# A graph layer and a sparse expert layer in one launch: first pairs in an order written out by hand, three scatter slots, and a pair placed in its gate's turn

## The reference

```
xn  = layernorm(x)
h   = xn @ W.T + b;  s1 = h @ a1;  s2 = h @ a2
att = sigmoid(s1[i] + s2[j] + att_b) * adj * mask[i] * mask[j]
att = att / (sum_j att + 1e-8)
x   = x + (att @ h) * mask
xn2 = layernorm(x)
w, e = softmax(top2(xn2 @ gate_w + gate_b))           # two of 16 experts
moe = sum over the two: w * (relu(xn2 @ w1[e] + b1[e]) @ w2[e] + b2[e])
out = x + layernorm(xn2 + moe) * gamma + beta
```

## Time and profile before

| | |
|---|---|
| median of 3 runs | 467.93 us (465.33 to 468.48) |
| span of the profiled execution | 466.4 us |
| its own time | not given apart from the span, which lies 1.5 us below the median |
| busy: PE, PEld, DVE, ACT, POOL | 341.8, 282.4, 304.0, 221.8, 311.9 us |
| first scatter, last scatter issued | 50.7, 213.8 us |
| first load of expert rows issued | 220.7 us |

### The profile page before, as it was taken

How to read it: one execution, slowest core, us unless ns; L and a number is a source line. 1 busy time by engine, 2 the same in 40 slices (tenths; PEclk the granted TensorE clock), 3 DMA queues, 4 the chain that set the end, 5 groups by cost and what they waited for, 6 DMA issues and landing times.

```text
span 466.4 us, 11731 instructions
## 1 busy us (share of the span) xinstructions
PE 341.8 (73%) x2259; PEld 282.4 (61%) x2259; DVE 304.0 (65%) x1456; ACT 221.8 (48%) x592; POOL 311.9 (67%) x346
## 2 busy tenths in 40 slices
PE   2787798978798826300799999888898899806991
PEld 1576677867797725200687777777777778702330
DVE  3989897986979948430366666666555555601985
ACT  2578798888889643300233334333333334501441
POOL 6642777777777777673177777777777777760565
PEclk9999998997979965555799999999999999955997
DMA  6912345544645632296867777778777776318983
GB/s 182 325 70 98 114 166 160 174 157 165 187 153 189 224 131 102 103 252 201 220 185 205 210 222 218 220 218 220 216 225 206 231 223 173 82 34 318 334 294 136
DMA packets 61962, 87.97 MB, mean 189 GB/s; under 512 B 10503, under 2 KB 41149, under 8 KB 61780
## 3 DMA queue, kind: packets, MB, share of 16 engines
q1 hardware_dynamic: 32660, 44.89, 33.7%
q0 software_dynamic: 10720, 25.32, 15.2%
q10 hardware_dynamic: 18528, 17.19, 12.4%
HBM read 55.61 MB, written 32.73 MB: 189 GB/s over the span
## 4 chain that ended last, share of the span: by engine, by line
PE 26%; ACTq 16%; DVE 15%; issue 13%; DMA 9%; ACT 9%; SPq 6%; POOL 3%; DVEq 1%; POOLq 0%
PE psum L1187 7%; ACTq L564 6%; ACTq L277 5%; PE psum L1176 5%; ACTq L276 5%; ACT hid L569 4%; DMA sorted_x<-xrow,rows 3%; PE psum L1092 3%; DMA out_dram<-z 2%; PE psum L1110 2%; DVE z L1016 2%; DMA w_sb<-w_dram 2%; ACT xn L520 2%; DVE xmid L729 1%; POOL sorted_x L414 1%
## 5 line engine op out<-in xcount | busy, mean ns | idle before, releaser
L436 POOL DMA_INDIRECT token_y<-yb,xb x143 | 143.4, 1002 | 60.2 <-issue 38.7
L414 POOL DMA_INDIRECT sorted_x<-xrow,rows x128 | 123.4, 964 | 41.7 <-issue 39.1
L569 ACT ACTIVATE hid<-psum,b_sb 128x256 f32<-128x256 f32 (+1 forms) x188 | 69.3, 419 | 140.2 <-PE psum L1176 60.0
L1187 PE MATMUL psum<-w_sb,hid 128*128 x572 | 83.2, 283 | 12.0 <-ACT hid L569 11.9
L1187 PEld LDWEIGHTS psum<-w_sb,hid 128*128 128x128 f32 x572 | 74.5, 191 | 22.0 <-issue 19.3
L1176 PE MATMUL psum<-xbT,w_sb 128*128 128x256 f32 (+1 forms) x376 | 81.9, 341 | 2.1 <-DVE xbT L966 1.9
L975 DVE TENSOR_TENSOR yb<-psum,b_bc 128x256 f32<-128x256 f32 x94 | 33.9, 360 | 62.8 <-PE psum L1187 51.2
L1176 PEld LDWEIGHTS psum<-xbT,w_sb 128*128 128x128 f32 x376 | 57.6, 193 | 7.6 <-DVE xbT L966 4.2
L1166 PE MATMUL psum<-ident_aug,xb 128*128 128x128 f32 x143 | 33.3, 290 | 23.2 <-DMA xb<-sorted_x 21.2
L980 DVE SCALAR_TENSOR_TENSOR yb<-yb,xb 128x128 f32<-128x128 f32 x143 | 46.5, 353 | 3.3
L966 DVE COPY xbT<-psum 128x256 f32<-128x256 f32 x94 | 33.2, 353 | 23.6 <-PE psum L1166 23.5
(11 more groups left out here) (163 smaller groups left out, 559.4 us busy)
## 6 DMA issues: line engine op xcount, KB each, us to landing
xb<-sorted_x SPq DMA_DIRECT2D x49, 258.0 KB
w_sb<-w_dram ACTq DMA_DIRECT2D x83, 128.0 KB
adj_in<-adj_dram SPq DMA_DIRECT2D x32, 256.0 KB
got<-token_y SPq DMA_DIRECT2D x16, 512.0 KB, 5.9
xb<-sorted_x SPq DMA_DIRECT2D x45, 129.0 KB
out_dram<-z ACTq DMA_DIRECT2D x16, 256.0 KB, 3.2
w_sb<-w_dram SPq DMA_DIRECT2D x27, 128.0 KB
xmid<-x_dram SPq DMA_DIRECT2D x6, 512.0 KB, 8.1
```

The source lines that it names most:

```text
L414: pool.indirect_dma_start(sorted_x, bass.IndirectOffsetOnAxis(ap=rows[:, slot, t, k:k + 1], axis=0), xrow[:, slot, k, t, :], None).then_in ...
L436: pool.indirect_dma_start(token_y, bass.IndirectOffsetOnAxis(ap=xb[:, q, t, TO:TO + 1].bitcast(I32), axis=0), yb[:, h, t, :], None, bounds ...
L569: last = act.activation(hid[:, u % RING, c, 0:n], psum[:, 2 + u % 2, c * BT:c * BT + n], ACT.Relu, bias=b1_sb[:, c, e])
L1187: last = mm(psum[:, 4 + u % 2, t * D:(t + 1) * D], hid[:, u % RING, c, t * P:(t + 1) * P], w2_sb[:, e, c * D:(c + 1) * D].rearrange("p a c ...
```

## The change

- **Weights.** The three vectors a1, a2 and b come as the columns of one array, b and att_b as one row: three loads instead of seven. b2 is loaded on a semaphore of its own, and its centring on PE (centre_b2) and copy on DVE (setup_b2) come later. w2 of experts 0 and 1 and chunk 3 of x are issued ahead of the gate and norm weights.
- **First pairs.** The first pairs have an order of their own on ACT, DVE and PE, written out, up to turn 3; from there on turns follow as before. The loops are written out on all four engines.
- **Later statistics.** Statistics of chunk 5 come behind attention of pair 1, those of 6 behind turn 3, of 7 and 8 behind turns 6 and 7. Scale and shift of chunks 5 to 8 are made by DVE, for two chunks at a time, with the Newton steps, behind turn 3 (after chunk 6) and turn 8.
- **Placing.** A pair's rank stands at the end of PE's turn in which its gate stands, and its row numbers and place are woven into the same turn's Newton steps on DVE. ACT weighs ahead of norm2.
- **Slots.** xrow and rows have three slots. POOL clears a part of each between the scales of the first chunks, and z uses the place of slot 0.

The diff, cut:

```diff
-LOOP_FROM, LOOP_TO = 4, PAIRS - 2
+POOL_X = 5
+XROWS = 3
...
-            for dst, src in ((w_raw[:, :], gnn_w), (vec[:, 0:1], gnn_a1.rearrange("(p a) -> p a", a=1)),
-                             (vec[:, 1:2], gnn_a2.rearrange("(p a) -> p a", a=1)),
-                             (vec[:, 2:3], gnn_b.rearrange("(p a) -> p a", a=1)),
-                             (h_bias[:, 0:D], gnn_b.rearrange("(a c) -> a c", a=1)),
-                             (att_b_sb[:, :], att_b.rearrange("(a c) -> a c", a=1)), (b2_raw, b2)):
+            for dst, src in ((w_raw[:, :], gnn_w), (vec[:, 0:3], gnn_cols),
+                             (h_bias[:, :], gnn_row.rearrange("(a c) -> a c", a=1))):
...
             load_adj(0)
+            load_w2(0, 0)
+            load_x(sp, EARLY_X)
+            load_w2(1, 1)
+            sp.dma_start(b2_raw, b2).then_inc(b2_raw_in, 16)
             for dst, src in ((gate_w_sb[:, :], gate_w), (gate_last[:, :], gate_w[D - 1, :].partition_broadcast(P)),
                              (gate_b_bc[:, :], gate_b.partition_broadcast(P)),
                              (gamma_bc[:, :], gamma.partition_broadcast(P)),
                              (beta_bc[:, :], beta.partition_broadcast(P))):
                 sp.dma_start(dst, src).then_inc(late_in, 16)
-            for c in range(EARLY_X, EARLY_X + 2):
-                load_x(sp, c)
-            for e in range(2):
-                load_w2(e, e)
-            for c in range(EARLY_X + 2, len(XCHUNKS)):
+            for c in range(EARLY_X + 1, len(XCHUNKS)):
                 load_x(sp, c)
...
-            for c in range(len(XCHUNKS)):
+            for c in range(POOL_X):
                 rstd1_of(c)
-            with pool.Fori(0, PAIRS // 2) as j:
-                for s in range(2):
-                    turn(2 * j + s, s)
+                if c < XROWS:
+                    clear_residuals(c)
+            for i in range(PAIRS):
+                turn(i, i % XROWS)
...
-            def keep(i, slot):
-                if begun(i, 2):
-                    act.wait_ge(scattered[slot], free_after(i, slot))
+            def keep(i):
+                slot = i % XROWS
+                act.wait_ge(res_clear, min(i + 1, XROWS))
+                if i >= XROWS:
+                    act.wait_ge(scattered[slot], free_after(i))
...
                     keep_h(m + 1, 1, 1 - slot)
-                    sigmoids(m + 1, 1 - slot)
+                    for p in range(2):
+                        sigmoids(m + 1, p, 1 - slot)
                 if valid(m + 2):
                     transposed(m + 2)
                 if valid(m - 2):
-                    keep(m - 2, slot)
+                    keep(m - 2)
+                    weigh(m - 2)
                 if valid(m - 1):
                     norm2(m - 1)
-                if valid(m - 2):
-                    weigh(m - 2, slot)
...
             norm1(0)
             transposed(0)
-            for m in range(-1, LOOP_FROM):
-                turn(m, m % 2)
-            with act.Fori(0, (LOOP_TO - LOOP_FROM) // 2) as j:
-                for s in range(2):
-                    turn(LOOP_FROM + 2 * j + s, (LOOP_FROM + s) % 2)
-            for m in range(LOOP_TO, PAIRS + 2):
-                turn(m, m % 2)
+            norm1(1)
+            for p in range(2):
+                keep_h(0, p, 0)
+                sigmoids(0, p, 0)
+            transposed(1)
+            norm1(2)
+            for p in range(2):
+                keep_h(1, p, 1)
+                sigmoids(1, p, 1)
+            transposed(2)
+            norm1(3)
+            norm2(0)
+            transposed2(0)
+            for p in range(2):
+                keep_h(2, p, 0)
+                sigmoids(2, p, 0)
+            transposed(3)
+            keep(0)
+            keep_h(3, 0, 1)
+            norm1(4)
+            keep_h(3, 1, 1)
+            for p in range(2):
+                sigmoids(3, p, 1)
+            transposed(4)
+            weigh(0)
+            norm2(1)
+            for m in range(3, PAIRS + 2):
+                turn(m)
...
+            def setup_b2():
                 dve.wait_ge(setup_pe, 4)
                 v.tensor_copy(b2_less, psum[0:EXPERTS, 7, 0:D]).then_inc(b2_ready, 1)
...
+            def place(i, n):
+                slot = i % XROWS
+                if i >= XROWS:
+                    dve.wait_ge(scattered[slot], free_after(i))
...
+            def rstd1_of(c):
+                lo, hi = XCHUNKS[c][0], XCHUNKS[c + 1][1]
+                dve.wait_ge(stats1, c + 2)
+                n = step(v.tensor_scalar(var_eps1[:, :], mv1[:, lo:hi, 1], EPS, -0.5, ALU.add, ALU.mult))
+                n = first_guess(half_bits(n, late), late)
+                for k in range(2):
+                    n = better_guess(k, times_variance(square(k, n, late), late), late)
+                n = better_guess(2, times_variance(square(2, n, late), late), late, out=rstd1[:, lo:hi])
+                dve.wait_ge(dve_step, n)
+                v.scalar_tensor_tensor(out=shift1[:, 1, lo:hi], in0=mv1[:, lo:hi, 0], scalar=-1.0, in1=rstd1[:, lo:hi],
+                                       op0=ALU.mult, op1=ALU.mult).then_inc(rstd1_late, (hi - lo) // TPP)
...
+            def norm_route_and_place(r, i):
+                n = largest(i)
+                r = half_bits(r)
+                n = which(i, n)
+                r = first_guess(r)
+                n = one_hot(n)
+                r = square(0, r)
+                choose(n)
+                r = times_variance(r)
+                r = better_guess(0, r)
+                r = square(1, r)
+                r = times_variance(r)
+                r = better_guess(1, r)
+                n = row_numbers(i)
+                r = square(2, r)
+                n = pick(n)
+                r = times_variance(r)
+                r = better_guess(2, r)
+                place(i, n)
+                shift2(r)
...
+            def turn(m):
+                residual(m - 1, graphs(m, 0) if valid(m) else ())
+                r = variance(m - 1, graphs(m, 1) if valid(m) else ())
+                norm_route_and_place(r, m - 2)
...
             stats_of(0)
             setup_weights()
+            setup_projection()
             stats_of(1)
-            setup_projection()
-            for c in (2, 3):
-                stats_of(c)
+            stats_of(2)
+            setup_b2()
             setup_gate()
+            stats_of(3)
+            attend_all(0)
             stats_of(4)
-            turn(0, 0)
-            for c in (5, 6):
-                stats_of(c)
-            turn(1, 1)
-            stats_of(7)
-            turn(2, 0)
-            stats_of(8)
-            per = steps[0]
-            turn(3, 1)
-            per = steps[0] - per
-            base = steps[0]
-            with dve.Fori(0, (LOOP_TO - LOOP_FROM) // 2) as j:
-                for s in range(2):
-                    steps[0] = base + j * (2 * per) + s * per
-                    turn(LOOP_FROM + 2 * j + s, (LOOP_FROM + s) % 2)
-            steps[0] = base + per * (LOOP_TO - LOOP_FROM)
-            for m in range(LOOP_TO, PAIRS + 3):
-                turn(m, m % 2)
+            residual(0)
+            norm(variance(0))
+            attend_all(1)
+            stats_of(5)
+            residual(1)
+            r = variance(1)
+            attend_all(2)
+            norm_route_and_place(r, 0)
+            turn(3)
+            stats_of(6)
+            rstd1_of(5)
+            for m in range(4, PAIRS + 1):
+                turn(m)
+                if m in (6, 7):
+                    stats_of(m + 1)
+                if m == 8:
+                    rstd1_of(7)
+            route_and_place(PAIRS - 1)
...
+            def centre_b2():
+                pe.wait_ge(b2_raw_in, 16)
+                mm(psum[0:EXPERTS, 7, 0:D], b2_raw, centre, start=True, stop=True).then_inc(setup_pe, 1)
...
-                if valid(m - 3):
-                    rank(m - 3)
                 if valid(m - 2):
-                    transpose_x2(m - 2, m + 2 if not isinstance(m, int) else min(m + 2, PAIRS))
+                    transpose_x2(m - 2, min(m + 2, PAIRS))
                 if valid(m + 1):
                     project_s1(m + 1)
                     project(m + 1, 1, 1 - slot)
@@ -1139,16 +1193,38 @@
                     transpose_x(m + 2)
                 if valid(m):
                     aggregate(m, slot)
+                if valid(m - 2):
+                    rank(m - 2)
...
             transpose_x(0)
             transpose_adj(0)
-            for m in range(-1, LOOP_FROM):
-                turn(m, m % 2)
-            with pe.Fori(0, (LOOP_TO - LOOP_FROM) // 2) as j:
-                for s in range(2):
-                    turn(LOOP_FROM + 2 * j + s, (LOOP_FROM + s) % 2)
-            for m in range(LOOP_TO, PAIRS + 3):
-                turn(m, m % 2)
+            project(0, 0, 0)
+            project_s1(0)
+            project(0, 1, 0)
+            transpose_x(1)
+            centre_b2()
+            aggregate(0, 0)
```

(76 more changed lines are left out.)

210 lines of the change are left out of this document (79 added, 131 removed).

## The result

The changed kernel took 461.25 us (median of 4, 460.26 to 466.18), the kernel before 468.14 beside it: ratio 0.9893, 95% interval 0.9857 to 0.9930. The prediction was 463.3. Beside the last experiments it was measured once more: 460.42 against 466.99, ratio 0.9864 (0.9839 to 0.9890). So it is faster by 1.1% and 1.4%, clear of no change, and by less than 2%. Rows and figures of "after" are those of the first profile, span 459.2 (466.4 before), 460.95 us in all. One run in the table further down, of e67_stats3_and_w1_on_act, was slow (473.15 us at a granted clock of 0.72) and is in no median here.

The account below looks back on a forecast made before the run. Bound: the later of SP's queue behind the last pair and POOL's last scatter, releasing the first expert-row load. 220.67 - 216.1 (middle of both) is 4.6, taken from the median 467.93: 463.3 us; range 458.5 to 470.5.

Parts of the forecast that it names:

- both arms: End of first stage: SP's queue (first load at 216.0 us) and POOL's last scatter (214.0 to 216.2) release the load.
- steps 1 to 6: Start of first stage: weights 6.0 us, w_aug 10.1, b2's copy 17.6, pair 0 placed at 45.0 against 49.73.
- step 4: Start: DVE's added stop in setup_b2 for PE's b2 product; 17.9 us at the worst, 17.6 taken.
- Rival (b): Start gains nothing: pair 0 at 49.7 us, last pair at 195.6, time 467.9; chance 0.22 together with Rival (d).
- the sum: Last pair's placing: 45.2 + 9.2 + 10.25 + 7.95 + 13 x 9.1 = 190.9 us, against 195.59 before.
- the loop: Turns: DVE's shift2, ScalarE's norm2, PE's transposes, gate, then DVE's route, norm and place: 8.85 us, level with DVE's 8.82.
- The fall of the clock: Turns: 0.25 us a turn, 3.3 over 13, taken for one fall of PE's clock.
- Signs of being wrong: Pair 0 placed later than 48 us, clock 0.5 in more than one turn, rank or gate waits over 1 us at full clock.
- step 6: Start, norm_route_and_place of pair 0: 3.9 us, and some 2 more waiting for rank; pair 0 placed at 45.0.
- POOL's arm: First stage's scatters: first at 46.0 us, last issue ends at 211.1 or 213.3, load released at 214.0 to 216.2.
- Rival (d): POOL's arm bounds, with 5 us for written-out code: load at 219 to 221, time 466 to 468; 0.22 with Rival (b).
- Rival (a): PE's clock falls after inserted statistics: three more falls, 12 us, last pair at 203, time 475.2; chance 0.14.

Follow-up runs that it names:

- e67_stats3_and_w1_on_act: Changed kernel with chunk 3's statistics moved ahead of b2's rearrangement on DVE and the first eleven w1 loads issued by ScalarE instead of SP: 457.62 us, ratio 0.9794.

## Why the prediction was right

**The bound.** Right: both arms matter, SP's is the later, 245 us behind the first load stay. The arms stood some 1.6 us apart (213.92 and, with SP's queue emptied, 212.29), which I had as 0 to 2. In the repeat they were level: 212.25 by SP and, as an estimate, 212.2 by POOL (last issue's end at 208.68, and 3.48 from there to the load as in the kernel with w1 on ScalarE). The gain, forecast as 4.6 us, came as 6.9 and 6.6: the mechanism held, and its size was a third too small.

**The start, steps 1 to 6.** Weights at 5.25 (6.0 predicted), w_aug 8.99 to 9.28 (10.1), the added wait 3.50 and b2's copy at 16.53 (17.6), rank's wait 1.89 (2), pair 0 placed at 44.27 (45.0), first scatter 45.47 (46.0). The mechanism of each step was right, and each was a little long (step 4's own terms, 15.1 and 3, make 18.1, where it has 17.9 at the worst; 16.53 was measured). Rival (b) falls. What I missed lies in step 4: I counted what is queued behind the added wait, and did not ask which of it could stand ahead. The experiment that does so gains 2.9 us at the start.

**The turns.** Turn 3 took 9.20 as said. The 13 turns from 53.54 took 126.35, where the sum has 128.55 with the later statistics in it: 2.2 too long. The statistics and scales cost 9.8 (their four turns took 44.88, four undisturbed ones 35.09), where I had 10.25. The rest is 8.97 a turn, where I had 9.1. Undisturbed turns took 8.68 to 8.93 (8.85 predicted from the loop), with waits of at most 0.46 for the gate: the loop and DVE's work are level, as the step has it. The fall of the clock that I spread over the turns came in the last two (10.61 and 9.45) and in the last gate, so the last pair took 9.09 instead of 7.95. In sum 188.98 against 190.9: 0.9 from the start, 2.2 from the turns, 1.1 back in the last pair.

**Signs of being wrong.** Two that I had named did come. The granted clock was 0.50 in more than one turn: in turn 4 and in the last two. And DVE waited more than 1 us for a rank at full clock, 1.89 for the first, which step 6 has in its sum. The fall in turn 4 cost nothing that its length shows, the late one 2.5 us in two turns and 1.1 in the last pair, where 3.3 was taken.

**Three slots** removed every wait for a scatter, as predicted (the repeat has one, of 0.64 us); the runs put their worth at 0.8 to 1.3% on the kernel before and 0.9% in the changed one. That DVE leads POOL by less than two pairs held here, and fell where statistics no longer slow DVE and where POOL starves early.

**POOL's arm.** Last issue ends at 209.07 against 211.1: 0.5 from the start, 0.8 from a starving of 1.84 instead of 2.6, and 0.7 from the one at pair 7, which didn't come. From the last issue's end to the load I had 2.9; the kernel with w1 on ScalarE took 3.48. Rival (d) falls: scatters take 960 ns in the median in both.

**Rival (a)** falls too. Of the four blocks of statistics and scales on DVE only the first was followed by 1.2 GHz, and turn 4 was 4.4 us over an undisturbed one, where its statistics and steps account for 4.9. Its premise, that PE has nothing to do meanwhile, hardly held for the other three. PE's timeline of the changed kernel, behind the first block, behind the second, and in a turn without any:

```profile
61.26 1.57 PE L1147 MATMUL psum<-h_sb,att 128*128 128x129 f32 x8 [2.45 <-DVE att L713]
...
86.16 0.66 PE L1155 MATMUL psum<-ident_aug,xn 128*128 128x128 f32 x4 [1.40 <-ACT xn L532]
...
117.79 0.66 PE L1155 MATMUL psum<-ident_aug,xn 128*128 128x128 f32 x4 [1.40 <-ACT xn L532]
```

Behind the other three blocks PE waited 1.39 to 1.40 us, as in turns without any (1.30 to 1.40), and 0.51 to 0.71 later on for an attention. Behind the first it waited 1.45, and 2.45 more for an attention. The rule of the Trainium skill quoted in the prediction (TensorE: Matmul & The Clock Gate, HAM oscillation — how this bites in real kernels) speaks of a PE that is left waiting, so the last three blocks hardly test it. The rows agree with it for the first.

**What is left open:** whether the w1 loads on ScalarE cost the second stage something. Behind the first load two of the four kernels with them took 247.4 and 247.6 us, the other two 245.8 and 245.9, and all other profiles 244.2 to 247.0. One profile each does not tell it from scatter. Open too is why the kernel before with its loops written out was 0.5% slower.

## What to carry to other kernels

Where two arms end a stage within a few us, price every edit on both: here the same reordering was worth little to the last pair and 3 us to the queue of scatters, because of when the first and second pairs were placed. When a change adds a wait on an in-order engine, look for work queued behind it that needs nothing from it and put that ahead: it gained half as much again as the whole change. Price a wait for a buffer by the arm that ends the stage and not by its length: with early statistics DVE waited 3.57 us for a slot at no cost, since POOL, which frees the slots, held the end.

## What was unexpected of the hardware

POOL's unexplained pause of 2.17 us inside the last pairs' scatters stands in all four profiles with two slots, each time ahead of the second scatter of the 15th pair, and in none of the ten with three. POOL's timeline of the changed kernel with two slots:

```profile
192.07 0.97 POOL L419 DMA_INDIRECT sorted_x<-xrow,rows  x1 [2.10 <-issue]
```

And of the kernel before with its loops written out, still with two slots:

```profile
195.73 0.97 POOL L415 DMA_INDIRECT sorted_x<-xrow,rows  x1 [2.37 <-issue]
```

Nothing that the profile shows releases it. It is some 2 us on POOL's arm; why it comes, and why it goes with the third slot, is not settled.
